# Four column tiles of 32 for the sums and the router's products, and the queries' high part on ScalarE

## Chip, cores and metric

The kernel runs on 1 core of a Trainium2 chip. The metric is the device time of one execution in microseconds (us), lower is better. Its engines are TensorE (PE; PEld is its weight load), VectorE (DVE), ScalarE (ACT), GpSimd (POOL) and SyncE (SP), which here issues most DMAs. Each engine runs its own instructions in program order and waits for the others through semaphores.

## The reference, cut to what matters

```python
# x, ctx: (4, 512, 512); 8 heads over the 512 positions, d = 64 positions each
xn  = layernorm(x)
q, k = l2norm over d of xn and ctx, per head
sm  = softmax(5.0 * einsum('bhdq,bhdk->bhqk', q, k))
x   = x + einsum('bhqk,bhdk->bhdq', sm, v)          # v = ctx
t   = layernorm(x).reshape(2048, 512)
logits = t @ Wg + bg                                 # 4 experts
# top 2 of 4, each expert keeps its 512 best tokens;
# out[sel] += (gelu(tok @ W1[i]) @ W2[i]) * p   for each expert i
return x + out
```

## The kernel before

The work has two phases. The attention phase goes through 16 units of 128 rows of `x` (two heads each). The expert phase (four experts, FP32 products made of three FP32R products of high and low parts) follows after a stretch that finds each expert's tokens. The change touches the attention phase alone.

A unit u passes through the engines in a software pipeline. In the body `unit(u, behind, ahead)` of each engine stand steps of units u-3 to u+3, written in a fixed order by hand; units 4 to 11 are a hardware loop of two bodies, the others are unrolled. `behind` and `ahead` say how many units lie before and after, up to 4 and 3. In the middle the orders are:

- PE: transpose the context of u+1 into `bank_t` (`values`, L1246), transpose the widened query norms of u+1 into `bank_m` (`spread_queries`, L1254), scores of u for key tiles 2 and 3 (L1267), weighted values 0 and 1 (L1277), transpose the normalized rows of u+2 into `bank_m`, transpose `x2n` of u-3 into `bank_t`, scores of u+1 for tiles 0 and 1, router logits of u-3 (L1305: four products, each with 128x128 weights `x2n_t` and 4 moving columns `wg`, into `bank_t`), weighted values 2 and 3, sums (L1289: four products of `half_sum` against 64 columns of ones, heads at rows 0 and 64 of `o_ps[1]`, two accumulated for each head).
- DVE: statistics of u+3, `queries(u+1)` (L823 `q_f`, L825 `q_hi`, then `x_norm` of u+2 at L788, then `q_lo` at L831), key squares of u+1, half sums 0, `invert_few(u-1)` (L844), query squares of u+2, half sums 1, residual and second statistics of u-2, `widen_queries(u+2)` (L837), `take_logits(u-3)` (L815), `normalize_x2(u-2)` (L892, waits for `rstd2` of POOL).
- ACT: sums of u-1 (L673), key squares and values of u+1 (L626, L633), four exponentials of u for tiles 2 and 3 (L653), query squares of u+2 (L618), `x2n_t` of u-3 (L679), four exponentials of u+1 for tiles 0 and 1, which wait for the key norms of POOL, key high part of u+2 (L643), output of u (L665).
- POOL: key norms of u+1, query norms of u+2, two inverse deviations, key low part.
- SP, in a ring over the unit: store `x2n` (L402), load `x_all` (L372) and `c_sb` (L377), two DMAs `few` (L410: one row of `p_sum` for each head, spread over 64 partitions of 8), wait for `few_inv` of DVE, store it to `inv_dram` (L412), two broadcasts back into `p_inv` (L415), store the output rows (L399, waits for DVE's residual).

`values(u+1)` on PE waits for `logit_done` (of u-4) in the middle units, since the logits stood in `bank_t`; `spread_queries` follows it.

Of the kernel before, what the change touches and what calls it, by code (L numbers as in the profile page):

```python
# [15 lines left out]
ALU = mybir.AluOpType  # L16
# [22 lines left out]
FEW = 2 * D // P  # L39
DVE_HEADS, POOL_HEADS = (0, 1), ()  # L40
# [28 lines left out]
C_ALL = C_RESET + E * 2 * UNITS  # L69


def constants():

    import numpy as np

    c = np.zeros((P, C_ALL), np.float32)
    p = np.arange(P)
    c[:, C_IDENT:C_IDENT + P] = np.eye(P)
    c[:, C_BEFORE:C_BEFORE + P] = (p[:, None] < p[None, :]) - 1.0
    c[:, C_ONES:C_ONES + P] = 1  # L80
    c[:, C_BLOCK:C_BLOCK + P] = p[:, None] // WAYS == p[None, :] // WAYS
# [8 lines left out]
    c[:, C_RESET:C_ALL] = np.arange(E * 2 * UNITS) % (2 * UNITS) != 0  # L90
    return c


def xattn_moe_kernel(nc, x, ctx_in, Wg, bg, W1, W2, consts, out):
# [6 lines left out]
    with ExitStack() as stack:  # L101
# [8 lines left out]
        wg = keep("wg", [P, KD, E])  # L110
# [59 lines left out]
        with ExitStack() as phase:  # L170
            def att(name, shape, dt=F32):
                return phase.enter_context(nc.sbuf_tensor(name, shape, dt))

            x_all = att("x_all", [P, UNITS, D])
            c_sb = [att(f"c_sb{n}", [P, D]) for n in range(2)]
            c_sq = att("c_sq", [P, D])
            x_norm = [att(f"x_norm{n}", [P, D]) for n in range(2)]
            x_sq = att("x_sq", [P, D])

            k_hi = [att(f"k_hi{n}", [P, D], F32R) for n in range(2)]  # L180
            k_lo = [att(f"k_lo{n}", [P, D], F32R) for n in range(2)]
# [8 lines left out]
            few = att("few", [P, FEW])  # L190
# [4 lines left out]
            x2n_t = att("x2n_t", [P, KD, P])  # L195
            stats = att("stats", [P, 6])
# [12 lines left out]
            wide_q = att("wide_q", [P, TT, 2, DH])  # L209
            power = att("power", [P, 16])  # L210
# [26 lines left out]
        wg_in = sem("wg_in")  # L237
        bg_in = sem("bg_in")
# [33 lines left out]
        few_in = sem("few_in")  # L272
        few_done = sem("few_done")
# [95 lines left out]
        def _(sp):  # L369
# [23 lines left out]
            sp.dma_start(wg[:, :, :], Wg.rearrange("(k p) e -> p k e", p=P)).then_inc(wg_in, 16)  # L393
# [10 lines left out]
            def spread_inverse(u):  # L404
# [3 lines left out]
                for h in range(2):  # L408
                    half = slice(h * P // 2, (h + 1) * P // 2)
                    sp.dma_start(few[half, :], p_sum[DH * h:DH * h + 1, :]).then_inc(few_in, 16)  # L410
# [63 lines left out]
        def _(pool):  # L474
# [3 lines left out]
            nc.gpsimd.memset(power[:, :], -0.5).then_inc(power_set, 1)  # L478
            pool.wait_ge(power_set, 1)
# [131 lines left out]
        def _(act):  # L611
# [32 lines left out]

            def exponentials(u, t, reused):
# [21 lines left out]
            def take_sums(u, reused):  # L667
# [3 lines left out]
                if reused:  # L671
                    act.wait_ge(few_in, 32 * n)
                nc.scalar.activation(p_sum[:, :], o_ps[1][:, :], ACT.Copy).then_inc(sum_taken, 1)  # L673

            def take_x2t(u, bank=bank_t):
# [4 lines left out]
                                     ACT.Copy).then_inc(x2t_taken, 1)  # L680

# [12 lines left out]
            round_keys((0, 1), False)  # L694
            act.wait_ge(rk_done, 1)
# [3 lines left out]
            def unit(u, behind, ahead):  # L699
# [5 lines left out]
                exponentials(u, 2, behind > 0)  # L705
                exponentials(u, 3, behind > 0)
# [4 lines left out]
                if ahead:  # L711
                    act.wait_ge(rk_done, number(u) + 2)
                    exponentials(after(u), 0, True)
                    exponentials(after(u), 1, True)
                if ahead > 1:
# [55 lines left out]
        def _(dve):  # L771
# [39 lines left out]
            def take_logits(u, bank=bank_t):  # L811
# [4 lines left out]
                                        bank[:, 0:E], bgb[:, :], ALU.add).then_inc(logit_done, 1)  # L816

            def queries(u, follow):
# [151 lines left out]
            def unit(u, behind, ahead):  # L970
# [27 lines left out]
                if behind > 2:  # L998
                    take_logits(before(before(before(u))))
# [15 lines left out]
            take_logits(before(before(end)))  # L1015
# [11 lines left out]
            take_logits(end)  # L1027
# [206 lines left out]
        def _(pe):  # L1234
# [46 lines left out]
            def sums(u, behind, ahead):  # L1281
# [5 lines left out]
                for n in range(2):  # L1287
                    for h in range(2):
                        last = nc.tensor.matmul(o_ps[1][DH * h:DH * (h + 1), :], cst[:, C_ONES:C_ONES + DH],  # L1289
                                                half_sum[h][n][:, :], start=(n == 0), stop=(n == 1))  # L1290
# [10 lines left out]
            def router_logits(u, bank=bank_t):  # L1301
# [18 lines left out]
            def unit(u, behind, ahead):  # L1320
# [16 lines left out]
                if ahead > 1:  # L1337
                    pe.wait_ge(qhi_done, n + 2)
                    transpose_queries(after(after(u)))
                if behind > 2:  # L1340
                    if ahead:
                        pe.wait_ge(v_taken, n + 2)
                    else:
                        pe.wait_ge(logit_done, n - 3)
# [26 lines left out]
            router_logits(before(before(end)))  # L1371
# [3 lines left out]
            router_logits(before(end), bank_m)  # L1375
            pe.wait_ge(logit_done, UNITS - 2)
            transpose_x2(end)
            router_logits(end)
# [126 lines left out]
```

## Time and profile before

| | us |
|---|---|
| median of 3 runs | 624.82 |
| lowest, highest | 622.26, 625.44 |
| the profiled execution, whole | 624.58 |
| its span, first to last instruction | 622.8 |
| mean granted TensorE clock in it | 0.957 of full |
| attention phase, roughly | 0 to 200 |
| expert phase, roughly | 262 to 622 |

The rows below come from the one profiled execution. Times are counted from the span's start. An engine's next short instruction can start a little before the last one's recorded end, so distances are taken from start to start. A row of the timeline that ends in a bracket tells how long the engine sat idle before it and what ended that. The name written `logits` in a row of DVE is `take_logits`.

### The profile page before, as it was taken

How to read it: one execution, taken by the hardware profiler on the slowest of the kernel's cores; microseconds unless marked ns; L12 is line 12 of the kernel's file. 1: busy time of each engine (PE TensorE's matmuls, PEld its weight loads, DVE VectorE, ACT ScalarE, POOL GpSimd, SP SyncE). 2: the span in 40 equal slices, each digit the busy share in tenths (PEclk: the TensorE clock that was granted, in tenths of full speed). 3: DMA queues.
4: the chain of work that ended last, by engine and by line, in shares of the span. 5: the costliest groups of instructions: out<-in, count | busy, mean ns of one | idle time of the engine just before them, and what ended most of it. 6: DMA issues, size and time to landing. Idle time of an engine off the chain costs nothing.

```text
span 622.8 us, 8726 instructions
## 1 busy us (share of the span) xinstructions
PE 568.2 (91%) x2842; PEld 408.5 (66%) x2842; DVE 354.3 (57%) x702; ACT 281.6 (45%) x421; POOL 187.0 (30%) x143
## 2 busy tenths in 40 slices
PE   3999999999998512999999999999999999999994
PEld 2545554554554401788888888888888788888883
DVE  5789998999888684443345443444633354423212
ACT  3777767767777130443333433334334324333220
POOL 8456566566551243100120330300510400500002
PEclk9999999999999655799999999999999999999998
DMA  4523423323213133323332543324451432542001
GB/s 146 196 60 119 137 86 118 126 94 109 96 53 118 52 115 96 95 100 128 97 113 88 183 149 120 118 84 134 152 184 69 137 124 76 190 149 68 0 1 67
DMA packets 46600, 67.73 MB, mean 109 GB/s; under 512 B 8560, under 2 KB 25072, under 8 KB 46576
## 3 DMA queue, kind: packets, MB, share of 16 engines
q1 hardware_dynamic: 42736, 54.84, 26.4%
q0 software_dynamic: 3840, 12.59, 6.2%
q8 instruction: 13, 0.21, 0.1%
q14 instruction: 11, 0.09, 0.0%
HBM read 54.70 MB, written 12.64 MB: 108 GB/s over the span
## 4 chain that ended last, share of the span: by engine, by line
PE 65%; DVE 5%; issue 4%; DMA 1%; POOL 1%; POOLq 0%; DVEq 0%; ACT 0%; SPq 0%
PE two L1423 29%; PE four L1453 9%; PE four L1452 9%; PE four L1450 9%; PE two L1277 2%; PE four L1267 2%; DVE junk L1046 1%; PE two L1289 1%; PE bank_t L1305 1%; DMA x_got<-x2n_dram,idx_all 1%; POOL w_lo L533 1%; DMA p_inv<-inv_dram 0%; PE bank_t L1411 0%; PE bank_m L1411 0%; DVE onehot L1133 0%
## 5 line engine op out<-in xcount | busy, mean ns | idle before, releaser
L759 ACT ACTIVATE h_f<-two 128x512 f32<-128x512 f32 x64 | 38.3, 599 | 231.2 <-PE two L1423 231.2
L1207 DVE TENSOR_TENSOR h_lo<-h_f,h_hi 128x512 fp32r<-128x512 f32 x64 | 44.1, 689 | 125.7 <-ACT h_hi L760 125.7
L1423 PE MATMUL two<-xt_hi,w_hi 128*128 (+1 forms) x256 | 102.9, 402 | 0.7 <-ACT xt_hi L748 0.7
L1423 PE MATMUL two<-xt_hi,w_lo 128*128 (+1 forms) x256 | 101.3, 396 | 0.0
L1453 PE MATMUL four<-w_hi,h_lo 128*128 128x512 f32 x256 | 100.5, 393 | 0.0
L1423 PE MATMUL two<-xt_lo,w_hi 128*128 (+1 forms) x256 | 100.5, 395 | 0.0
L1450 PE MATMUL four<-w_hi,h_hi 128*128 128x512 f32 x256 | 100.5, 392 | 0.0
L1452 PE MATMUL four<-w_lo,h_hi 128*128 128x512 f32 x256 | 100.4, 392 | 0.0
L653 ACT ACTIVATE prob<-four,rnorm 128x512 f32<-128x512 f32 x128 | 77.6, 688 | 28.6 <-POOL rnorm L476 17.6
L1177 DVE TENSOR_TENSOR w_lo<-raw,w_hi 128x2048 fp32r<-128x2048 f32 x30 | 68.7, 2290 | 23.3 <-ACT w_hi L686 23.3
L476 POOL TENSOR_TENSOR rnorm<-ss_max,power 128x8 f32<-128x8 f32 x32 | 64.7, 2024 | 51.5 <-DVE ss_max L808 45.3
L606 POOL DMA_INDIRECT out<-o_got,idx_all x16 | 20.2, 1264 | 165.4 <-DVE o_got L1228 163.0
L585 POOL DMA_INDIRECT x_got<-x2n_dram,idx_all x16 | 23.9, 1496 | 139.9 <-DVE idx_all L1164 125.1
L1277 PE MATMUL two<-prob,v_t 128*64 128x512 f32 x256 | 62.0, 605 | 0.0
L686 ACT ACTIVATE w_hi<-raw 128x2048 fp32r<-128x2048 f32 x32 | 61.3, 1918 | 0.0
L1423 PEld LDWEIGHTS two<-xt_hi,w_hi 128*128 128x128 f32 x256 | 48.6, 190 | 11.7 <-ACT xt_hi L748 1.1
L1423 PEld LDWEIGHTS two<-xt_hi,w_lo 128*128 128x128 f32 x256 | 48.6, 190 | 11.1
L1423 PEld LDWEIGHTS two<-xt_lo,w_hi 128*128 128x128 f32 x256 | 48.5, 189 | 10.7
L1450 PEld LDWEIGHTS four<-w_hi,h_hi 128*128 128x128 f32 x256 | 48.1, 188 | 10.9
L1453 PEld LDWEIGHTS four<-w_hi,h_lo 128*128 128x128 f32 x256 | 48.1, 188 | 10.8
L1452 PEld LDWEIGHTS four<-w_lo,h_hi 128*128 128x128 f32 x256 | 48.1, 188 | 10.6
L856 DVE TENSOR_TENSOR half_sum<-prob 128x512 f32<-128x512 f32 x64 | 41.5, 689 | 0.1
(177 smaller groups left out, 741.5 us busy)
## 6 DMA issues: line engine op xcount, KB each, us to landing
raw<-in_L_ffn_W SPq DMA_DIRECT2D x64, 512.0 KB, 4.0
x_all<-in_x SPq DMA_DIRECT2D x16, 256.0 KB, 2.9
c_sb<-in_ctx SPq DMA_DIRECT2D x16, 256.0 KB, 2.8
out<-x_all SPq DMA_DIRECT2D x16, 256.0 KB, 2.0
x2n_dram<-x2n SPq DMA_DIRECT2D x16, 256.0 KB, 2.0
p_inv<-inv_dram SPq DMA_DIRECT2D x30, 128.0 KB, 2.8
few<-p_sum SPq DMA_DIRECT2D x30, 2.0 KB, 2.2
cst<-in_consts SPq DMA_DIRECT2D x1, 354.5 KB, 5.0
```

Source lines behind the costliest of these rows:

```text
L476: return nc.gpsimd.tensor_tensor(dst, src, power[:, 0:n], ALU.pow)
L653: last = nc.scalar.activation(prob[h][t][:, :], s_ps[:, 2 * (t % 2) + h, :], ACT.Exp, scale=rnorm[u[1]][:, 0, t, h:h + 1])
L686: nc.scalar.activation(w_hi[c % SPLIT_BUFS][:, :], raw[c % RAW_BUFS][:, :], ACT.Copy).then_inc(whi_done, 1)
L759: nc.scalar.activation(h_f[m % 2][:, :], z_ps[m % 2][:, :], ACT.Gelu)
L856: nc.vector.tensor_tensor(half_sum[h][n][:, :], prob[h][2 * n][:, :], prob[h][2 * n + 1][:, :], ALU.add).then_inc(halves_done[h], 1)
L1177: nc.vector.tensor_tensor(w_lo[c % SPLIT_BUFS][:, :], raw[c % RAW_BUFS][:, :], w_hi[c % SPLIT_BUFS][:, :].bitcast(F32), ALU.subtract).then ...
L1207: nc.vector.tensor_tensor(h_lo[m % 2][:, :], h_f[m % 2][:, :], h_hi[m % 2][:, :].bitcast(F32), ALU.subtract).then_inc(h_split, 1)
L1277: last = nc.tensor.matmul(o_ps[0][DH * h:DH * (h + 1), :], v_t[u[1]][:, t, h, :], prob[h][t][:, :], start=(t == 0), stop=(t == TT - 1))
L1423: return nc.tensor.matmul(z[:, :], w_part[c][:, w], x_k, start=start, stop=stop)
L1450: nc.tensor.matmul(acc_ps[:, t, :], h_hi[m % 2][:, h], w_hi[c][:, w], start=(m == 0), stop=False)
L1452: nc.tensor.matmul(acc_ps[:, t, :], h_hi[m % 2][:, h], w_lo[c][:, w], start=False, stop=False)
L1453: last = nc.tensor.matmul(acc_ps[:, t, :], h_lo[m % 2][:, h], w_hi[c][:, w], start=False, stop=(m == MT - 1))
```

## The change

Three things are changed in the attention phase:

1. In units with `ahead`, the four sum products go to four column tiles of 32 (rows 0, 32, 64, 96 of `o_ps[1]`) with nothing accumulated. So each head has two partial sums: SP issues four `few` DMAs for two, DVE adds the two halves of `few` and then inverts.
2. The router's logits of the middle units: weights and moving data are swapped (`wg`, widened with zeros to 32 columns, is the weight, `x2n_t` moves, 128 columns), the four parts stand on four column tiles of `bank_m`; ACT copies them (`r_part`, 128x128), and one more product with the constant `C_QUAD` adds and transposes them into `bank_m`. They are placed around the sums, at the end of PE's body. `values` then waits for `x2t_taken`, and `spread_queries` for `logit_done`. In the last units the four products stay as they were (`router_whole`).
3. `q_hi` is no longer computed by DVE from `x_norm`: ACT copies `q_f`, between the exponentials of tiles 2 and 3. DVE normalizes u+2 before it waits for it.

```diff
@@ SP
-            sp.dma_start(wg[:, :, :], Wg.rearrange("(k p) e -> p k e", p=P)).then_inc(wg_in, 16)
+            sp.wait_ge(wg_clear, 1)
+            sp.dma_start(wg[:, :, 0:E], Wg.rearrange("(k p) e -> p k e", p=P)).then_inc(wg_in, 16)
...
                 for h in range(2):
                     half = slice(h * P // 2, (h + 1) * P // 2)
-                    sp.dma_start(few[half, :], p_sum[DH * h:DH * h + 1, :]).then_inc(few_in, 16)
+                    for m in range(2):
+                        row = QUAD * (2 * m + h)
+                        sp.dma_start(few[half, m * FEW:(m + 1) * FEW], p_sum[row:row + 1, :]).then_inc(few_in, 16)
@@ POOL
+            nc.gpsimd.memset(wg[:, :, :], 0.0).then_inc(wg_clear, 1)
@@ ACT
+            def round_queries(u):
+
+                act.wait_ge(q_done, number(u) + 1)
+                nc.scalar.activation(q_hi[u[1]][:, :], q_f[:, :], ACT.Copy).then_inc(qhi_done, 1)
+            def take_parts(u, bank=bank_m):
+
+                act.wait_ge(parts_ready, number(u) + 1)
+                nc.scalar.activation(r_part[:, :], bank[:, 0:P], ACT.Copy).then_inc(parts_taken, 1)
...
                 exponentials(u, 2, behind > 0)
+                if ahead:
+                    round_queries(after(u))
                 exponentials(u, 3, behind > 0)
...
                     exponentials(after(u), 1, True)
+                if behind > 2 and ahead:
+                    take_parts(before(before(before(u))))
@@ DVE
-                nc.vector.scalar_tensor_tensor(q_hi[u[1]][:, :], x_norm[u[1]][:, :], ALPHA, bank_m[:, :],
-                                               ALU.mult, ALU.mult).then_inc(qhi_done, 1)
+                if follow is not None:
+                    normalize(follow)
                 dve.wait_ge(q_done, n + 1)
                 dve.wait_ge(qhi_done, n + 1)
-                if follow is not None:
-                    normalize(follow)
                 nc.vector.tensor_tensor(q_lo[u[1]][:, :], q_f[:, :], q_hi[u[1]][:, :].bitcast(F32), ALU.subtract
                                         ).then_inc(q_split, 1)
...
-                dve.wait_ge(few_in, 32 * (n + 1))
-                nc.vector.reciprocal(few_inv[:, :], few[:, :]).then_inc(few_done, 1)
+                dve.wait_ge(few_in, 64 * (n + 1))
+                nc.vector.tensor_tensor(few_sum[:, :], few[:, 0:FEW], few[:, FEW:2 * FEW], ALU.add
+                                        ).then_inc(few_added, 1)
+                dve.wait_ge(few_added, n + 1)
+                nc.vector.reciprocal(few_inv[:, :], few_sum[:, :]).then_inc(few_done, 1)
@@ PE
+                        if ahead:
+
+                            row = QUAD * (2 * n + h)
+                            last = nc.tensor.matmul(o_ps[1][row:row + QUAD, :], cst[:, C_ONES:C_ONES + QUAD],
+                                                    half_sum[h][n][:, :], start=True, stop=True,
+                                                    tile_position=(0, row))
...
+            def router_parts(u, bank=bank_m):
 
                 pe.wait_ge(x2t_taken, number(u) + 1)
                 for k in range(KD):
-                    last = nc.tensor.matmul(bank[:, 0:E], x2n_t[:, k, :], wg[:, k, :],
+                    last = nc.tensor.matmul(bank[QUAD * k:QUAD * (k + 1), 0:P], wg[:, k, :], x2n_t[:, k, :],
+                                            start=True, stop=True, tile_position=(0, QUAD * k))
+                last.then_inc(parts_ready, 1)
+
+            def router_logits(u, bank=bank_m):
+
+                pe.wait_ge(parts_taken, number(u) + 1)
+                nc.tensor.matmul(bank[:, P:P + E], r_part[:, :], cst[:, C_QUAD:C_QUAD + E], start=True, stop=True
+                                 ).then_inc(logit_ready, 1)
...
                 if ahead:
                     if behind > 3:
-                        pe.wait_ge(logit_done, n - 3)
+                        pe.wait_ge(x2t_taken, n - 3)
                     else:
                         pe.wait_ge(v_taken, n + 1)
                     values(after(u))
+                    if behind > 3:
+                        pe.wait_ge(logit_done, n - 3)
                     spread_queries(after(u))
...
-                    pe.wait_ge(qhi_done, n + 2)
+                    pe.wait_ge(q_done, n + 2)
                     transpose_queries(after(after(u)))
...
-                if behind > 2:
-                    router_logits(before(before(before(u))))
+                if not ahead:
+                    router_whole(before(before(before(u))), bank_t)
                 weighted_values(u, 2)
                 weighted_values(u, 3)
+                if behind > 2 and ahead:
+                    pe.wait_ge(xsq_done, n + 3 if ahead > 1 else UNITS)
+                    router_parts(before(before(before(u))))
                 sums(u, behind, ahead)
+                if behind > 2 and ahead:
+                    router_logits(before(before(before(u))))
```

## Rows read from the trace of the kernel before

**Rows 1.** Windows: length, busy us (count) of PE, PEld, DVE, ACT, POOL; clock, DMA share, GB/s.
```profile
60.50:155.50 95.00, 93.90 (x580) 50.66 (x576) 86.58 (x218) 69.01 (x120) 57.23 (x40) 1.00 0.34 112
262.00:622.00 360.00, 351.95 (x1595) 286.63 (x1593) 142.79 (x152) 122.29 (x155) 55.66 (x40) 0.99 0.33 111
```

**Rows 2.** Timeline of DVE, one unit: start us, us, what, count, idle before.
```profile
120.21 0.16 DVE L815 TENSOR_TENSOR logits<-bank_t,bgb 128x4 f32 x1
...
120.83 0.55 DVE L892 TENSOR_SCALAR x2n<-x_all,mv,rstd 128x512 f32 x1 [0.47 <-POOL rstd L476]
...
122.31 0.68 DVE L823 SCALAR_TENSOR_TENSOR q_f<-x_norm,bank_m 128x512 f32<-128x512 f32 x1
122.91 0.68 DVE L825 SCALAR_TENSOR_TENSOR q_hi<-x_norm,bank_m 128x512 fp32r<-128x512 f32 x1
...
124.14 0.68 DVE L831 TENSOR_TENSOR q_lo<-q_f,q_hi 128x512 fp32r<-128x512 f32 x1
...
126.87 0.19 DVE L844 RECIPROCAL few_inv<-few 128x8 f32<-128x8 f32 x1
...
127.82 1.30 DVE L856 TENSOR_TENSOR half_sum<-prob 128x512 f32<-128x512 f32 x2
...
131.95 0.15 DVE L815 TENSOR_TENSOR logits<-bank_t,bgb 128x4 f32 x1
```

**Rows 3.** The same view, the unit before it.
```profile
108.20 0.15 DVE L815 TENSOR_TENSOR logits<-bank_t,bgb 128x4 f32 x1
...
112.42 0.68 DVE L831 TENSOR_TENSOR q_lo<-q_f,q_hi 128x512 fp32r<-128x512 f32 x1
```

**Rows 4.** Timeline of PE around the same unit.
```profile
115.59 1.05 PE L1305 MATMUL bank_t<-wg,x2n_t 128*128 128x4 f32 x8
...
118.34 1.89 PE L1289 MATMUL two<-half_sum,cst 128*64 128x512 f32 x8
120.50 0.65 PE L1246 MATMUL bank_t<-cst,c_sb 128*128 128x128 f32 x4 [0.27 <-DVE logits L815]
120.98 0.60 PE L1254 MATMUL bank_m<-cst,wide_q 128*128 128x128 f32 x4
121.51 0.51 PE L1267 MATMUL four<-q_hi,k_hi 64*128 64x512 f32 x2
```

**Rows 5.** Timeline of ACT in the same unit.
```profile
118.76 0.65 ACT L643 ACTIVATE k_hi<-c_sb 128x512 fp32r<-128x512 f32 x1
...
122.74 2.42 ACT L653 ACTIVATE prob<-four,rnorm 128x512 f32<-128x512 f32 x4 [0.47 <-PE four L1267]
...
128.18 2.42 ACT L653 ACTIVATE prob<-four,rnorm 128x512 f32<-128x512 f32 x4 [1.41 <-POOL rnorm L476]
```

**Rows 6.** Timeline of SP's DMA issues, both units.
```profile
111.52 1.14 SPq L410 DMA_DIRECT2D few<-p_sum  x2
...
123.29 1.13 SPq L410 DMA_DIRECT2D few<-p_sum  x2
```

**Rows 7.** Tile `few`, 60 to 156 us: issue ns min/median/max; DMA from issue to landing.
```profile
L410 SPq DMA_DIRECT2D few<-p_sum x16: 491/548/597, 64.2 to 147.6; - x16
...
DMA to landing us min/median/max: 2.0/2.3/2.5
```

**Rows 8.** The same tile, 168 to 192 us, where no inputs are loaded.
```profile
DMA to landing us min/median/max: 1.7/1.8/1.8
```

**Rows 9.** Timeline of DVE: first and last logits of the loop, the last units.
```profile
60.89 0.15 DVE L815 TENSOR_TENSOR logits<-bank_t,bgb 128x4 f32<-128x4 f32 x1
...
155.68 0.15 DVE L815 TENSOR_TENSOR logits<-bank_t,bgb 128x4 f32 x1
...
178.17 0.15 DVE L815 TENSOR_TENSOR logits<-bank_t,bgb 128x4 f32<-128x4 f32 x1
...
181.72 0.69 DVE L831 TENSOR_TENSOR q_lo<-q_f,q_hi 128x512 fp32r<-128x512 f32 x1
```

**Rows 10.** Timeline of ACT in a unit before the first logits.
```profile
45.52 1.84 ACT L653 ACTIVATE prob<-four,rnorm 128x512 f32<-128x512 f32 x3 [0.81 <-POOL rnorm L476]
```

More of the change, by code:

```diff
@@ L39 @@
 FEW = 2 * D // P
+QUAD = P // 4
 DVE_HEADS, POOL_HEADS = (0, 1), ()
@@ L68 @@
 C_RESET = C_SELF + E * E
-C_ALL = C_RESET + E * 2 * UNITS
+C_QUAD = C_RESET + E * 2 * UNITS
+C_ALL = C_QUAD + E
 def constants():
@@ L89, in constants @@
     c[:, C_SELF:C_SELF + E * E] = (j == i) * -1e30
-    c[:, C_RESET:C_ALL] = np.arange(E * 2 * UNITS) % (2 * UNITS) != 0
+    c[:, C_RESET:C_QUAD] = np.arange(E * 2 * UNITS) % (2 * UNITS) != 0
+    c[:, C_QUAD:C_ALL] = p[:, None] % QUAD == np.arange(E)[None, :]
     return c
@@ L109, in xattn_moe_kernel @@
         cst = keep("cst", [P, C_ALL])
-        wg = keep("wg", [P, KD, E])
+        wg = keep("wg", [P, KD, QUAD])
         bgb = keep("bgb", [P, E])
@@ L189, in xattn_moe_kernel @@
             half_sum = [[att(f"half_sum{h}{n}", [P, D]) for n in range(2)] for h in range(2)]
-            few = att("few", [P, FEW])
+            few = att("few", [P, 2 * FEW])
+            few_sum = att("few_sum", [P, FEW])
             few_inv = att("few_inv", [P, FEW])
@@ L195, in xattn_moe_kernel @@
             x2n_t = att("x2n_t", [P, KD, P])
+            r_part = att("r_part", [P, P])
             stats = att("stats", [P, 6])
@@ L237, in xattn_moe_kernel @@
         wg_in = sem("wg_in")
+        wg_clear = sem("wg_clear")
+        parts_ready = sem("parts_ready")
+        parts_taken = sem("parts_taken")
         bg_in = sem("bg_in")
@@ L272, in xattn_moe_kernel @@
         few_in = sem("few_in")
+        few_added = sem("few_added")
         few_done = sem("few_done")
@@ L671, in take_sums @@
                 if reused:
-                    act.wait_ge(few_in, 32 * n)
+                    act.wait_ge(few_in, 64 * n)
                 nc.scalar.activation(p_sum[:, :], o_ps[1][:, :], ACT.Copy).then_inc(sum_taken, 1)
@@ L694, in _ @@
             round_keys((0, 1), False)
+            round_queries((0, 0))
             act.wait_ge(rk_done, 1)
@@ L809, in sum_key_squares, with take_logits @@
                                         ).then_inc(ssk_floor, 1)
-            def take_logits(u, bank=bank_t):
+            def take_logits(u, bank=bank_m):
                 n = number(u)
@@ L815, in take_logits @@
                 nc.vector.tensor_tensor(logits[:, bass.ds(n, 1), :].rearrange("p a e -> p (a e)"),
-                                        bank[:, 0:E], bgb[:, :], ALU.add).then_inc(logit_done, 1)
+                                        bank[:, P:P + E], bgb[:, :], ALU.add).then_inc(logit_done, 1)
             def queries(u, follow):
@@ L998, in unit @@
                 if behind > 2:
-                    take_logits(before(before(before(u))))
+                    take_logits(before(before(before(u))), bank_m if ahead else bank_t)
                 if behind > 1 and ahead:
@@ L1014, in _ @@
             normalize_x2(before(end), True)
-            take_logits(before(before(end)))
+            take_logits(before(before(end)), bank_t)
             residual(end, 1)
@@ L1026, in _ @@
             put(nc.vector.scalar_tensor_tensor(rest0[:, :], count0[:, :], -2.0, excess[:, :], ALU.mult, ALU.add))
-            take_logits(end)
+            take_logits(end, bank_t)
             dve.wait_ge(logit_done, UNITS)
@@ L1288, in sums @@
                     for h in range(2):
-                        last = nc.tensor.matmul(o_ps[1][DH * h:DH * (h + 1), :], cst[:, C_ONES:C_ONES + DH],
-                                                half_sum[h][n][:, :], start=(n == 0), stop=(n == 1))
+                        if ahead:
[3 more added lines that the diff above has]
+                                                    tile_position=(0, row))
+                        else:
+                            last = nc.tensor.matmul(o_ps[1][DH * h:DH * (h + 1), :], cst[:, C_ONES:C_ONES + DH],
+                                                    half_sum[h][n][:, :], start=(n == 0), stop=(n == 1))
                 last.then_inc(sums_ready, 1)
@@ L1299, in transpose_x2, with router_whole @@
                 last.then_inc(x2t_ready, 1)
-            def router_logits(u, bank=bank_t):
+            def router_parts(u, bank=bank_m):
                 pe.wait_ge(x2t_taken, number(u) + 1)
                 for k in range(KD):
-                    last = nc.tensor.matmul(bank[:, 0:E], x2n_t[:, k, :], wg[:, k, :],
+                    last = nc.tensor.matmul(bank[QUAD * k:QUAD * (k + 1), 0:P], wg[:, k, :], x2n_t[:, k, :],
[5 more added lines that the diff above has]
+                                 ).then_inc(logit_ready, 1)
+            def router_whole(u, bank):
+                pe.wait_ge(x2t_taken, number(u) + 1)
+                for k in range(KD):
+                    last = nc.tensor.matmul(bank[:, P:P + E], x2n_t[:, k, :], wg[:, k, 0:E],
                                             start=(k == 0), stop=(k == KD - 1))
@@ L1343, in unit @@
                     else:
-                        pe.wait_ge(logit_done, n - 3)
+                        pe.wait_ge(x2t_taken, n - 3)
                     transpose_x2(before(before(before(u))))
@@ L1370, in _ @@
             transpose_x2(before(before(end)))
-            router_logits(before(before(end)))
+            router_whole(before(before(end)), bank_t)
             pe.wait_ge(exp_done, TT * UNITS)
@@ L1374, in _ @@
             transpose_x2(before(end), bank_m)
-            router_logits(before(end), bank_m)
+            router_whole(before(end), bank_m)
             pe.wait_ge(logit_done, UNITS - 2)
             transpose_x2(end)
-            router_logits(end)
+            router_whole(end, bank_t)
             transpose_keys(EARLY, UNITS, 2)
```

## The prediction

> **What bounds the kernel now.** I read the table of windows first, then the timelines of DVE, PE, ACT and SP over two units of the loop. The change touches only the attention phase; the expert phase, 360 us at a granted clock of 0.99, stays [rows 1]. In 95 us of the loop PE is busy 93.9 us and DVE 86.6 us [rows 1], so the table alone says "PE". The timelines say something else. From one `take_logits` to the next on DVE is 12.01 and 11.74 us (108.20, 120.21, 131.95) [rows 2, 3], on average (155.68 - 60.89) / 8 = 11.85 us [rows 9]. PE's `values` starts 0.29 us after `take_logits` of DVE and had been idle 0.27 us for it [rows 4]. Behind `take_logits` DVE has no idle time but 0.47 us at `x2n` for POOL [rows 2]: the busy share of 91% hides gaps between dependent instructions. So two rings of nearly equal length hold each other. A saving on PE alone is worth nothing beyond that 0.27; the unit gets shorter only if the ring through DVE does.
>
> I call the start of `take_logits` D, the start of `q_lo` Q. Before, D to Q is 4.22 and 3.93 us, Q to the next D 7.79 and 7.81 us [rows 2, 3].
>
> **The change part by part.**
>
> *Sums on four column tiles.* Eight passes on two tiles take about 1.8 us from start to end [rows 4]; on four tiles I take half, 0.9 us; bounds 0.9 (four abreast) and 1.8 (two abreast as now). Saved on PE: 0 to 0.9 us a unit.
>
> *Router.* The old four products take 1.05 us on PE [rows 4]. New: eight passes of 128 columns on four tiles, then one product with 4 columns. One old product is a quarter of 1.05, 0.26; I take 0.35 + 0.3 us, bounds 0.4 and 1.3 in all. ACT gets one more copy of 128x128, at most the 0.65 us of a 128x512 copy such as `k_hi` [rows 5]; I take 0.3.
>
> Together PE falls from about 11.7 to 10.4 us a unit: it stops being a bound. But its logits now come last in its body. They must be there when DVE is at D. Half sums 1 of DVE end 2.8 us before D (127.82 + 1.30 against 131.95) [rows 2]; after them PE needs the sums and one product, 1.2 us (2.1 at the upper bounds): ready 0.7 to 1.6 us early. ACT's `take_parts` stands behind the exponentials of u+1, which start 4.04 us after Q (128.18 against 124.14) [rows 2, 5] and last 2.42; with the copy, the product and two hand-overs that is Q + 7.2, against Q + 8.0 for D: hidden as well, by 0.8 us. Nothing of parts 1 and 2 on PE costs or gains.
>
> *The wait of `spread_queries`.* `values` no longer waits for D; `spread_queries` does. So the chain from D is now: 0.29 us to the spread (the distance that D to `values` has now), 0.53 to the scores of tile 2 (120.98 to 121.51), 1.23 from there to the exponentials (121.51 to 122.74) [rows 4, 5]. The exponentials of tile 2 start at D + 2.05, where they were at D + 2.53.
>
> *`q_hi` on ACT.* DVE loses 0.60 us (122.31 to 122.91, q_f to q_hi) [rows 2]. But the copy stands behind the two exponentials of tile 2 on ACT. Two of four that last 2.42 us take 1.16 until the next can start, the copy like `k_hi` 0.65 [rows 5], the hand-over to DVE some 0.05. `q_hi` is there at 2.05 + 1.16 + 0.65 + 0.05 = D + 3.91. `q_f` ends at about D + 2.8 and `x_norm` at D + 3.3, so DVE is ready some 0.6 us too early and sits. D to Q becomes 3.91, in place of 4.22 and 3.93: of the 0.60 saved, 0.17 is left on average. Behind the waiting `q_lo` on DVE is the whole rest of the body, and behind Q POOL's key norms. The exponentials of tile 3 start 0.53 us later, which only WV 2 and 3 of PE and half sums 1 need, both microseconds later.
>
> *The addition of `few`.* One 128x8 instruction more and a wait for it: about 0.19 for such an instruction (`few_inv`) [rows 2], 0.20 with the gap. It lies on DVE's path. Q to D becomes 7.80 + 0.20 = 8.00. So far a unit is 3.91 + 8.00 = 11.91 us, against 11.85: nothing gained.
>
> *Two more `few` DMAs.* SP issues them behind the store of `x2n` and the two loads; the first `few` starts at D + 3.32 and D + 3.08 [rows 2, 3, 6]. One issue takes 0.49 to 0.60 us [rows 7] and two take 1.14 [rows 6], so the fourth starts 1.80 us after the first instead of 0.55. From issue to landing: 2.0 to 2.5 us in the loop [rows 7], 1.7 to 1.8 where no load is under way [rows 8]. The fourth comes as the loads are just ending, I take 2.0, bounds 1.7 and 2.5. All four are there at D + 3.32 + 3.80 = 7.12 and D + 6.88, and 0.05 for the wait. DVE stands at `invert_few` at Q + 2.73 (126.87 - 124.14) [rows 2], that is D + 6.64. It waits 0.53 and 0.29 us, 0.41 on average; bounds 0.1 and 0.9. Before, the second of two landed 0.7 us ahead of DVE. Nothing on DVE passes this wait: query squares, half sums 1, residual, `widen_queries` and D itself are behind it, and the next `x2n`, hence the next `few`, behind D. It closes a ring: 11.91 + 0.41 = 12.32 us a unit, +0.47.
>
> By "Issuing engines are not separate DMA queues" in *DMA: Bandwidth & Descriptors* of the Trainium skill, the time to initiate a DMA is usually small beside the DMA itself. Here an issue of 0.55 us stands against about 2 us; if it were nothing, the four would land with the second, no wait would arise, and the sum would be that of the first rival.
>
> *Edges.* The loop's eight distances: 8 x 0.47 = +3.8 us. The next unit still loads a context: +0.5. In the last two with logits there are no loads before `few`, so no wait for it, but DVE was not held by `q_hi` before: D to Q was 3.55 (178.17 to 181.72) [rows 9] and becomes 3.91, with the addition +0.56 each, 1.1 together. The tail behind them hangs on `few_inv` and is carried along. The first units have no logits. There a part of PE's saving could show (at most 3 x 0.9 us), yet their exponentials of u+1 already wait 0.81 us for POOL's norm [rows 10], which is behind Q, and Q moves back by about 1.1 us against the spread: I take +0.3, bounds -2 and +1. POOL's memset of `wg` and SP's wait for it: under 0.1 us beside loads, nothing.
>
> Sum: 3.8 + 0.5 + 1.1 + 0.3 = +5.7 us. The profiled execution took 624.58 us whole (622.8 span and 1.8 around it), 0.2 under the median: 624.6 + 5.7 = 630.3 us.
>
> **The rivals.**
> 1. *No wait for `few`.* The two later DMAs land in 1.7 us or less from issue, or issue faster. Then a unit is 11.91: 8 x 0.06 = 0.5, the next +0.3, +1.1 and +0.3: 626.8 us. For it: 1.7 where the queues are empty [rows 8]. Against it: `c_sb` is issued only 0.5 us before `few`, and landings in the loop are 2.0 and more [rows 7].
> 2. *A larger wait.* Four `few` of 64 small pieces each hold one another up in the queues, landing 2.5 us after issue: wait 0.9, a unit 12.8, 624.6 + 8 x 0.97 + 2.3 = 634.7 us.
> 3. *Faster.* The hold-up at `q_lo` is not there, because ACT comes to the exponentials of tile 2 earlier than my chain allows, and `few` is there in time. Then DVE's balance decides: -0.60 - 0.2 (the gap ahead of `x_norm` in every second unit, 0.1 on average) + 0.20, about -0.45 a unit over 12 units: 619 us. Against it: the chain D, spread, scores, exponentials, copy, `q_lo` is written out in program order on each engine, and every piece has a row. A reader of the busy table would go further and take off PE's whole 1.3 us a unit, 609 us; DVE's ring does not allow that. *TensorEngine Tiling (Array Packing)*, "Theoretical Speedup", of the Trainium skill promises up to 4x for 32 columns; by that rule and a PE bound it would be this 609. No row of the kernel before has four tiles.
> 4. *The tiles don't run abreast.* If the four 32-column products run one after another, the sums take 3.6 us rather than 0.9, with the product and its hand-overs 4.0 us behind half sums 1, logits are ready 1.2 us after DVE wants them, a unit is about 13.1: 624.6 + 12 x 1.25 = 640 us. It decides once sums and logits last over 2.8 us together. Against it: two tiles already overlap, eight passes recorded as 0.59 us each in 1.89 [rows 4].
>
> **How the numbers follow.** Forecast (few-wait of 0.2 to 0.7) 0.50; rival 1: 0.25; rival 2: 0.13; rival 3: 0.09; rival 4: 0.03. The likeliest gives 630.3. Its own range is 628 to 633 (wait bounds, and the edges). The range of 8 in 10 takes in rival 1 down to 625.5 and most of rival 2: 625.5 to 634.5. 0.5% is 3.1 us, about what a measurement of this kernel can tell from no change: slower means over 627.9. Slower: 0.50 less 0.03, 0.13, 0.03: 0.63. Faster, under 621.7: 0.09, and the rest 0.28 is within.
>
> **What would show it.** In the changed kernel: `take_logits` to `take_logits` near 12.3 us; ahead of `q_lo` DVE idle 0.5 to 0.7 us, released by ACT `q_hi`; ahead of `few_sum` idle 0.3 to 0.5, released by the DMA; PE busy less, with idle time ahead of `spread_queries`, released by DVE's logits; sums in 0.9 us. It is wrong if DVE has no idle time at `q_lo`, if PE waits for nothing, or if `take_logits` itself waits for PE.

## The result, and the profile after

| | before | changed |
|---|---|---|
| median, us | 623.81 (4 runs) | 630.18 (4 runs) |
| lowest, highest | 622.26, 625.44 | 629.30, 630.52 |
| span of the profiled execution | 622.8 | 628.4 |
| mean granted TensorE clock | 0.957 | 0.955 |

The ratio is 1.0101, 95% interval 1.0077 to 1.0125: slower by 1.0%. The forecast was 630.3 us. One execution among all those below, of the kernel with the sums alone, took 952.74 us at a mean granted clock of 0.559 of full and is left out of that kernel's figures.

The engines of the changed kernel, from its page (busy us, share of the span, instructions). Before, PE was busy 568.2 us, DVE 354.3 and ACT 281.6.

```profile
PE 556.8 (89%) x2866; PEld 395.9 (63%) x2866; DVE 348.1 (55%) x701; ACT 288.5 (46%) x449; POOL 187.1 (30%) x144
```

TensorE does 11.4 us less and VectorE 6.2 us less, and the kernel is 5.6 us longer. The next line is the loop in the table of windows, as [rows 1] show it of the kernel before. From the first to the last of the nine `take_logits` that bound eight units it takes 99.4 us, against 94.8 before, and PE is busy 88.9 us of it, against 93.7.

```profile
61.60:161.00 99.40, 88.90 (x592) 43.74 (x592) 83.64 (x217) 72.62 (x137) 57.15 (x41) 0.98 0.33 108
```

The timeline of DVE over one unit of the changed kernel, as [rows 2, 3] show it of the kernel before:

```profile
112.41 0.15 DVE L843 TENSOR_TENSOR logits<-bank_m,bgb 128x4 f32 x1
...
114.67 0.69 DVE L851 SCALAR_TENSOR_TENSOR q_f<-x_norm,bank_m 128x512 f32<-128x512 f32 x1
115.28 0.54 DVE L816 TENSOR_SCALAR x_norm<-x_all,mv,rstd 128x512 f32 x1
116.41 0.69 DVE L857 TENSOR_TENSOR q_lo<-q_f,q_hi 128x512 fp32r<-128x512 f32 x1 [0.59 <-ACT q_hi L661]
...
119.43 0.17 DVE L870 TENSOR_TENSOR few_sum<-few 128x8 f32<-128x8 f32 x1 [0.22 <-DMA few<-p_sum]
119.64 0.20 DVE L873 RECIPROCAL few_inv<-few_sum 128x8 f32<-128x8 f32 x1
...
124.72 0.15 DVE L843 TENSOR_TENSOR logits<-bank_m,bgb 128x4 f32 x1
```

Where `q_hi` was computed, DVE now sits idle 0.59 us for ACT's copy of it, and further down 0.22 us for the `few` DMAs. ACT in the same stretch shows why: the copy comes when two exponentials are through, and those had waited 1.09 us for PE's scores.

```profile
114.52 1.27 ACT L671 ACTIVATE prob<-four,rnorm 128x512 f32<-128x512 f32 x2 [1.09 <-PE four L1296]
115.68 0.63 ACT L661 ACTIVATE q_hi<-q_f 128x512 fp32r<-128x512 f32 x1
116.20 1.27 ACT L671 ACTIVATE prob<-four,rnorm 128x512 f32<-128x512 f32 x2
```

PE at the end of that unit, against [rows 4]: the parts on four tiles, the sums on four, the adding product, `values`, and the spread, which now waits 0.99 us for DVE's logits (0.47 us in the unit before).

```profile
121.22 0.43 PE L1341 MATMUL bank_m<-x2n_t,wg 128*32 128x128 f32 x8
121.99 1.07 PE L1321 MATMUL two<-half_sum,cst 128*32 128x512 f32 x8 [0.35 <-issue]
123.09 0.39 PE L1348 MATMUL bank_m<-cst,r_part 128*128 128x4 f32 x2
123.33 0.63 PE L1275 MATMUL bank_t<-cst,c_sb 128*128 128x128 f32 x4
124.95 0.63 PE L1283 MATMUL bank_m<-cst,wide_q 128*128 128x128 f32 x4 [0.99 <-DVE logits L843]
```

So TensorE's saving arrived as work saved, 0.8 us in the sums (1.07 for 1.89) and some 0.2 in the router (0.43 and 0.39 for 1.05), and became idle time, most of it ahead of the spread. A second ring, through SyncE, is about as long as that through the copy of `q_hi`. In the stretch of 112 to 125 us the chain that the profile follows back, at each step to what ended its wait, runs there: from `x2n` through SyncE's queue and the last of the four DMAs to `few_sum`. In order of time (start, us, what):

```profile
112.95 0.56 DVE x2n L921
113.52 0.34 SPq L412
...
115.82 0.51 SPq L422
...
117.64 1.77 DMA few<-p_sum
119.43 0.18 DVE few_sum L870
...
124.72 0.17 DVE logits L843
```

One unit of the loop, its first, is an outlier: 14.12 us from `take_logits` to `take_logits` (61.62 to 75.74), with a wait of 2.03 us at `few_sum`.

```profile
70.45 0.17 DVE L870 TENSOR_TENSOR few_sum<-few 128x8 f32<-128x8 f32 x1 [2.03 <-DMA few<-p_sum]
```

In the sum of differences, changed minus before, by the starts of `take_logits`:

| stretch | before | changed | difference | forecast |
|---|---|---|---|---|
| start to the first of the loop | 60.89 | 61.62 | +0.7 | +0.3 |
| the outlier unit | 11.79 | 14.12 | +2.3 | +0.5 |
| seven other units | 83.00 | 85.27 | +2.3 | +3.3 |
| next unit | 11.32 | 11.60 | +0.3 | +0.5 |
| next two | 21.08 | 21.77 | +0.7 | +1.1 |
| the rest | 434.70 | 434.05 | -0.6 | 0 |
| span | 622.78 | 628.43 | +5.6 | +5.7 |

### The profile page after: what moved, and what is told of

Read it like the earlier page. It is cut to its first block, busy times and chain, and to the rows that moved or that the text cites. A ratio compares the mean times of both kernels' runs of the same rounds, so it can differ in the third digit from the quotient of the medians.

```text
span 628.4 us, 8855 instructions
## 1 busy us (share of the span) xinstructions
PE 556.8 (89%) x2866; PEld 395.9 (63%) x2866; DVE 348.1 (55%) x701; ACT 288.5 (46%) x449; POOL 187.1 (30%) x144
## 4 chain that ended last, share of the span: by engine, by line
PE 62%; DVE 11%; issue 9%; POOL 7%; DMA 3%; ACT 3%; SPq 3%; POOLq 0%; DVEq 0%; ACTq 0%
PE two L1480 29%; PE four L1510 9%; PE four L1509 9%; PE four L1507 9%; POOL rnorm L488 3%; POOL rstd L488 2%; DMA few<-p_sum 2%; ACT prob L671 2%; SPq L422 2%; PE four L1296 1%; DVE q_lo L857 1%; DVE half_sum L885 1%; DVE junk L1075 1%; ACT q_hi L661 1%; DVE ss L833 1%
## 5 line engine op out<-in xcount | busy, mean ns | idle before, releaser
L671 ACT ACTIVATE prob<-four,rnorm 128x512 f32<-128x512 f32 x128 | 79.5, 692 | 42.6 <-POOL rnorm L488 19.2
L1480 PEld LDWEIGHTS two<-xt_hi,w_hi 128*128 128x128 f32 x256 | 48.6, 190 | 11.7 <-issue 1.1
```

The costliest lines, as they stand in the source:

```text
L671: last = nc.scalar.activation(prob[h][t][:, :], s_ps[:, 2 * (t % 2) + h, :], ACT.Exp, scale=rnorm[u[1]][:, 0, t, h:h + 1])
L1480: return nc.tensor.matmul(z[:, :], w_part[c][:, w], x_k, start=start, stop=stop)
```

## The experiments

My theory: DVE's ring sets the unit. From D (`take_logits`) to Q (`q_lo`) it is held by the copy on ACT, from Q to D by DVE's own work with the addition, now and then by the `few` DMAs; PE is no bound. The rivals: PE's saving does count and something else ate it; or the loss is all in the DMAs; or all in the copy. The fences below show the main lines of each edit, cut at "...". Each kernel ran beside the kernel before, and each ratio is against it.

### One part undone

**Part 1 undone**: two tiles, two DMAs, no addition.

```diff
-                    for m in range(2):
-                        row = QUAD * (2 * m + h)
-                        sp.dma_start(few[half, m * FEW:(m + 1) * FEW], p_sum[row:row + 1, :]).then_inc(few_in, 16)
+                    sp.dma_start(few[half, 0:FEW], p_sum[DH * h:DH * h + 1, :]).then_inc(few_in, 16)
...
-                nc.vector.tensor_tensor(few_sum[:, :], few[:, 0:FEW], few[:, FEW:2 * FEW], ALU.add
...
-                        if ahead:
+                        if False:
```

> The changed kernel with part 1 undone: sums on two tiles, two few DMAs, no addition on DVE; router and ScalarE copy as changed. Theory (DVE's ring, with few, sets the unit): the wait of DVE ahead of few_inv is gone and so is the addition of 0.20 us, though PE's sums take 1.8 us again instead of 1.0. take_logits to take_logits about 11.75 us in the loop (12.14 and one of 14.12 in the changed kernel), time 624.7 us (623.5 to 626). Rival (PE's saving did count, and something else was lost): 0.8 us more on PE a unit show, 12.9 us a unit, about 638 us.

Measured: 627.26 us (626.6 to 627.66), ratio 1.0051 (1.0030 to 1.0071). A unit of the loop is 11.85 us on average (62.53 to 157.31), not 12.42 as in the changed kernel, and DVE never waits for `few`: the rival's 12.9 is excluded. But the time is 2.6 us over my figure and outside my range. The loop begins 0.9 us later than in the changed kernel (62.53 against 61.62) and the last units with logits take 11.44 and 10.97 us where those of the changed kernel take 11.39 and 10.38. In these edges PE is a bound and its longer sums show: DVE waits 0.80 us for the adding product of PE ahead of the last of these `take_logits` (at 191.12 us), and 0.04 us in the changed kernel.

**Part 3 undone**: `q_hi` by DVE.

```diff
-                if follow is not None:
-                    normalize(follow)
+                nc.vector.scalar_tensor_tensor(q_hi[u[1]][:, :], x_norm[u[1]][:, :], ALPHA, bank_m[:, :],
+                                               ALU.mult, ALU.mult).then_inc(qhi_done, 1)
...
-                if ahead:
-                    round_queries(after(u))
```

> The changed kernel with part 3 undone: DVE computes q_hi again, sums and router as changed. Theory: DVE does 0.60 us more but no longer waits 0.6 us for ScalarE, take_logits to q_lo 4.22 and 3.93 us in turn (4.00 and 3.89 in the changed kernel), a unit about 12.1 us, time 629.5 us (628 to 631), so about as the changed kernel. Rival (moving q_hi off DVE is a gain of 0.6 us a unit): 12.7 us a unit, 637 us. Rival (the copy is the whole loss): 624 us.

Measured: 629.06 us (626.45 to 629.52), ratio 1.0069 (1.0045 to 1.0094). D to Q 4.21 and 3.93, a unit 12.31 and 11.99 us. In the loop, DVE with 0.60 us more to do takes just as long as DVE that waits for the copy:

```profile
121.14 0.15 DVE L840 TENSOR_TENSOR logits<-bank_m,bgb 128x4 f32 x1
125.07 0.68 DVE L856 TENSOR_TENSOR q_lo<-q_f,q_hi 128x512 fp32r<-128x512 f32 x1
127.84 0.17 DVE L869 TENSOR_TENSOR few_sum<-few 128x8 f32<-128x8 f32 x1
133.13 0.15 DVE L840 TENSOR_TENSOR logits<-bank_m,bgb 128x4 f32 x1
```

**Part 2 undone**: the router and the wait of `values` as before.

```diff
-                        pe.wait_ge(x2t_taken, n - 3)
+                        pe.wait_ge(logit_done, n - 3)
...
                     values(after(u))
-                    if behind > 3:
-                        pe.wait_ge(logit_done, n - 3)
```

> The changed kernel with part 2 undone: the four router products as before, values waits for logit_done again; sums and ScalarE copy as changed. Theory: the queries' spread starts 0.78 us after take_logits instead of 0.29, so the exponentials and the copy behind them come 0.5 us later: take_logits to q_lo 4.4 us, a unit 12.4 us, few is there in time, time 632 us (630.5 to 634): the router's part is the one that helps. Rival (the router's extra copy and product cost something): 628 us or less.

Measured: 633.98 us (633.38 to 634.11), ratio 1.0160 (1.0134 to 1.0186). D to Q 4.40 to 4.42, every unit 12.41 to 12.43 us. DVE's wait at `q_lo` grows from 0.66 to 1.17 us, by as much as the spread comes later (it starts 0.78 us after D, not 0.29):

```profile
124.03 0.16 DVE L841 TENSOR_TENSOR logits<-bank_t,bgb 128x4 f32 x1
128.43 0.69 DVE L855 TENSOR_TENSOR q_lo<-q_f,q_hi 128x512 fp32r<-128x512 f32 x1 [1.17 <-ACT q_hi L661]
131.17 0.15 DVE L868 TENSOR_TENSOR few_sum<-few 128x8 f32<-128x8 f32 x1
```

In its profile the loop is as long as that of the changed kernel, 99.4 us: each unit is 0.24 us longer than a usual one there (12.42 for 12.18), 1.9 us over eight units, but it has no outlier. What the two profiles differ by lies outside the loop, most of it in the last three units with logits (36.15 us for 33.37), and 1.03 us of that is a wait for `few` (at 169.16 us), so not all of it is the spread.

### One part alone

These are the kernel before with one part of the change, made by undoing the two others as in the diffs above (for the router's part undone, the four old products and their place too).

> Part 1 alone on the kernel before: four column tiles for the sums, four few DMAs, the addition; router and q_hi as before. Theory: PE's saving shows only in the first units (about -0.8 us), then a unit is 4.08 + 8.00 = 12.08 us (11.85 before), and 0.2 us more in each of the last: 626.5 us (625 to 628). Rival (PE bound before): 12 x 0.8 less, 615 us.

Measured: 628.10 us (627.7 to 629.01), ratio 1.0068 (1.0048 to 1.0088). The loop begins at 59.74 us (60.89 before), then a unit is 12.18 us on average. PE is busy 0.7 us a unit less in the loop (88.0 us of eight units for 93.7) and the unit gets longer, not shorter: PE did not bound the loop of the kernel before. The addition and, in single units, a wait for `few` (0.32, and 1.00 in one of the last) cost more than I had allowed, 1.6 us over my figure and just outside my range.

> Part 2 alone on the kernel before: router parts on four tiles, the copy and the adding product; sums and q_hi as before. Theory: DVE's ring is unchanged, 11.85 us a unit; time 623.5 us (622 to 625), no difference that can be told. Rival (PE bound before): 0.4 us a unit less, 619 us. Rival (logits late at the end of PE's body): DVE idle ahead of take_logits, over 627 us.

Measured: 625.03 us (623.47 to 625.57), ratio 1.0012 (1.0000 to 1.0025). That is at the upper end of my range, 0.03 us outside it. A unit stays at 11.85 us. The router's products are recorded 0.2 us shorter, but PE's busy time in the loop hardly falls (93.57 us for 93.69), so this run alone says little on what PE's time is worth; the sums alone say it. The logits at the end of PE's body do hold up DVE in the last two units, where it has little to do:

```profile
177.32 0.16 DVE L838 TENSOR_TENSOR logits<-bank_m,bgb 128x4 f32<-128x4 f32 x1 [0.89 <-PE bank_m L1342]
188.28 0.16 DVE L838 TENSOR_TENSOR logits<-bank_m,bgb 128x4 f32<-128x4 f32 x1 [2.20 <-PE bank_m L1342]
```

> Part 3 alone on the kernel before: ScalarE copies q_hi between the exponentials; sums and router as before. Theory: without the earlier spread of part 2 the exponentials start 2.53 us after take_logits, q_lo at 4.4 us, a unit 12.2 us, and the first units later by 1.5 us: 632 us (630 to 633.5), the one part that costs most. Rival (0.6 us less for DVE is a gain): 620 us or less.

Measured: 630.25 us (629.56 to 631.22), ratio 1.0096 (1.0075 to 1.0117); D to Q 4.42 and 4.53, a unit 12.21 and 12.35 us. In medians the three alone cost 3.8, 0.7 and 5.9 us, 10.4 together, each against a median of 624.33; the whole change costs 6.4. The difference is part 2: alone it gives nothing, beside the copy it brings the spread forward and gives back about 4 us. The run with part 1 undone shows it in the loop: with parts 2 and 3 a unit is 11.85 us, with the copy alone 12.32. The run with part 2 undone costs 3.8 us more than the changed kernel.

### Is TensorE a bound in the changed kernel?

```diff
-                for n in range(2):
+                for n in (0, 1, 0, 1) if ahead else range(2):
```

> The changed kernel with the four sum products on PE issued twice over (same result, PE 0.9 to 1.0 us longer in each unit with ahead). Theory (PE is no bound in the changed kernel, its logits are ready about 1 us before DVE takes them): 630.2 us, within 1.5 us. Rival (PE counts): 12 units by 0.9 us, 641 us.

Measured: 631.35 us (630.02 to 632.05), ratio 1.0117 (1.0100 to 1.0134), where the changed kernel had 1.0101. The sums take 1.92 us instead of 1.07, and the spread's wait for DVE falls from 0.99 to 0.22 us:

```profile
123.08 1.92 PE L1321 MATMUL two<-half_sum,cst 128*32 128x512 f32 x16 [0.36 <-issue]
124.94 0.39 PE L1348 MATMUL bank_m<-cst,r_part 128*128 128x4 f32 x2
125.18 0.64 PE L1275 MATMUL bank_t<-cst,c_sb 128*128 128x128 f32 x4
126.04 0.64 PE L1283 MATMUL bank_m<-cst,wide_q 128*128 128x128 f32 x4 [0.22 <-DVE logits L843]
```

A unit is 12.32 and 12.01 us, as before the doubling. 0.85 us a unit of PE's time are free in the loop. What the doubling costs lies at the edges, where the loop begins at 63.26 us (61.62) and DVE waits 0.44 us for PE at the last `take_logits` of these units. The outlier is there again, in the same unit: 13.58 us with a wait of 1.49 us for `few`.

### Is it the place of the copy?

One step later on ACT, behind the exponentials of tile 3:

```diff
                 exponentials(u, 2, behind > 0)
-                if ahead:
-                    round_queries(after(u))
                 exponentials(u, 3, behind > 0)
+                if ahead:
+                    round_queries(after(u))
```

> The changed kernel with ScalarE's copy q_hi one step later, behind the exponentials of tile 3. Theory (the place of the copy on ScalarE sets q_lo): take_logits to q_lo goes from 3.95 to 5.1 us, a unit to 13.1 us, few in time, time about 640 us (637 to 643). Rival (q_lo's wait is covered by slack elsewhere): within 1 us of 630.

Measured: 644.48 us (two executions, 643.52 and 645.44), ratio 1.0333 (1.0312 to 1.0354). D to Q 5.15 and 5.06, a unit 13.14 and 13.08 us: D to Q is longer by 1.15 and 1.17 us, and two exponentials take 1.16 [rows 5]. The time is 4.5 us over my figure and outside my range; nearly all of it lies in the first units, which I had not counted: the loop begins at 65.53 us, not at 61.62.

```profile
117.97 0.15 DVE L843 TENSOR_TENSOR logits<-bank_m,bgb 128x4 f32 x1
123.11 0.69 DVE L857 TENSOR_TENSOR q_lo<-q_f,q_hi 128x512 fp32r<-128x512 f32 x1 [1.73 <-ACT q_hi L661]
```

### Is it the two more DMAs?

SyncE issues `few` behind the store of the output rows, ahead of the `x2n` store and the loads.

```diff
+                if follow is not None:
+                    issue_few(follow)
                 sp.wait_ge(x2n_done, n + 1)
                 sp.dma_start(x2n_dram[bass.ds(n * P, P), :], x2n[u[1]][:, :]).then_inc(x2n_stored[u[1]], 16)
```

> The changed kernel, but SyncE issues the four few DMAs before the store of x2n and the two loads. Theory: the wait ahead of few_sum is gone (0.22 us in every second unit, and the one of 2.03 us), every unit about 11.95 us, time 627.5 us (626.5 to 629): the two longer DMAs cost 2.5 to 3 us of the 6, the rest is the addition and the wait for q_hi. Rival (the few DMAs are the whole loss): 624.5 us. Rival (later loads stall something else): over 630 us.

Measured: 627.38 us (626.89 to 627.92), ratio 1.0058 (1.0038 to 1.0079). There is no wait at `few_sum` in any unit, nor an outlier: all are 11.91 to 12.00 us. By the ratios, 1.0058 and 1.0101, the place of the DMAs costs about 0.4% of the 1.0%. Single `few` land late here too (2.88 and 3.37 us), and DVE waits for none of them: issued early, they have the time.

```profile
121.59 0.15 DVE L851 TENSOR_TENSOR logits<-bank_m,bgb 128x4 f32 x1
125.48 0.69 DVE L865 TENSOR_TENSOR q_lo<-q_f,q_hi 128x512 fp32r<-128x512 f32 x1 [0.65 <-ACT q_hi L669]
128.22 0.15 DVE L878 TENSOR_TENSOR few_sum<-few 128x8 f32<-128x8 f32 x1
133.50 0.15 DVE L851 TENSOR_TENSOR logits<-bank_m,bgb 128x4 f32 x1
```

### A version that beats both

If the place of the copy is what holds DVE, then the copy ahead of the exponentials of tile 2 should let it go:

`few` stays first.

```diff
+                if ahead:
+                    round_queries(after(u))
                 exponentials(u, 2, behind > 0)
-                if ahead:
-                    round_queries(after(u))
                 exponentials(u, 3, behind > 0)
```

> few first as in the run of that name, and ScalarE's copy q_hi ahead of the exponentials of tile 2 instead of between them. It then starts when q_f is done, at 2.9 us after take_logits, and q_lo at 3.6 us. Theory: a unit about 11.65 us, time 624 us (622.5 to 626), about that of the kernel before. Rival (the exponentials, 1.4 us later, hold up PE or the next exponentials): 627 us or more.

Measured: 619.51 us (618.66 to 620.85), ratio 0.9931 (0.9918 to 0.9945): 0.7% faster than the kernel before. D to Q is 3.55 and 3.72, a unit 11.57 and 11.72 us, 11.62 on average, as expected. ACT now waits for `q_f` and not DVE for the exponentials; DVE's idle time ahead of `q_lo` is 0.31 us.

```profile
108.34 0.63 ACT L669 ACTIVATE q_hi<-q_f 128x512 fp32r<-128x512 f32 x1 [1.89 <-DVE q_f L859]
108.88 2.41 ACT L679 ACTIVATE prob<-four,rnorm 128x512 f32<-128x512 f32 x4
```

It is 4.5 us faster than my figure and outside my range, and that is again the edges: the loop begins at 58.95 us (61.80 with `few` first alone) and the last two units with logits take 10.38 and 9.95 us (11.39 and 10.38). The copy first without `few` first was not run.

The same with part 1 undone as above:

> The same with part 1 undone: two tiles, two few DMAs, no addition. Theory: 0.20 us less on DVE's ring, a unit about 11.45 us, time 621.5 us (620 to 623.5), faster than the kernel before by about 0.5%. Rival (with two tiles PE's 11.3 us of work are again the bound, or the tiles were worth it): 624 us or more.

Measured: 621.62 us (621.42 to 623.22), ratio 0.9970 (0.9960 to 0.9980). The number is as expected, but its reason is in part the rival: DVE now waits for PE's logits in every unit, 0.17 to 0.50 us.

```profile
118.79 0.16 DVE L849 TENSOR_TENSOR logits<-bank_m,bgb 128x4 f32 x1 [0.31 <-PE bank_m L1351]
```

A unit is 11.54 us on average. With DVE's ring shortened PE is the bound of the loop, busy in all of it. The loop with two tiles and that with four, in the table of windows:

```profile
61.01:153.35 92.34, 92.34 (x595) 45.15 (x595) 82.33 (x209) 73.72 (x137) 57.39 (x41) 1.00 0.35 115
58.95:151.92 92.97, 85.97 (x592) 43.02 (x592) 82.98 (x217) 71.82 (x138) 57.14 (x41) 1.00 0.36 115
```

In the loop four tiles don't pay even here: 11.62 us a unit for 11.54, with PE 6.4 us less busy and DVE's addition in its place. As whole kernels the ratios are 0.9931 (0.9918 to 0.9945) with four tiles and 0.9970 without, and that gain is in the edges: the loop begins 2.1 us earlier (58.95 for 61.01), and the last two units with logits take 10.38 and 9.95 us for 11.39 and 10.96.

And with part 2 undone instead:

> The version with few first and the copy ahead of tile 2's exponentials, with part 2 undone (router and the wait of values as before). Theory: the copy now starts when DVE's q_f is done, no matter when the exponentials could start, so the earlier spread is worth nothing: a unit 11.65 us, 620 us (618.5 to 621.5), as the version with part 2 (619.5). Rival (part 2 is needed for PE or the spread): 623 us or more.

Measured: 620.86 us (619.42 to 621.54), ratio 0.9941 (0.9918 to 0.9964), a unit 11.56 and 11.71 us. With the copy first, the earlier spread is worth nothing in the loop. Its interval overlaps that of the version with part 2 (0.9918 to 0.9945), so these runs don't tell whether part 2 gives anything there. A version with the copy first and both parts 1 and 2 undone was not run.

## Why the prediction was right, point by point

- **Two rings of nearly equal length, and PE's saving worth nothing in the loop.** Right. PE's work fell less than forecast: the sums took 1.07 us for a forecast 0.9, the router 0.43 and 0.39 for 0.35 and 0.3, and PE's busy time in a usual unit fell from 11.7 to 11.0 us, where I had 10.4. That it was worth nothing in the loop held: the sums alone made the loop longer, and sums twice over changed nothing in it. "Theoretical Speedup" in *TensorEngine Tiling (Array Packing)* of the Trainium skill allows up to 4x for 32 columns and up to 2x for 64, so up to twice as fast from one to the other. The trace comes near it: 1.07 against 1.89 us, 1.8 times.
- **D to Q 3.91 us.** Right: 3.89 to 3.90 in every second unit and 3.98 to 4.00 in the others, but for 4.20 in the one behind the outlier. The step that I took most care over, from the spread through the scores and two exponentials to the copy, held with each piece; the later copy added the two exponentials and the earlier one took them off. In the others the spread starts 0.06 us later after D (112.41 to 112.70 against 124.72 to 124.95) and the exponentials 0.10 later; I had one figure for both kinds of unit.
- **Q to D 8.00 us.** Right: with `few` first, where nothing waits at `few_sum`, it is 8.02 us (125.48 to 133.50). In the changed kernel it is 5.29 us from `few_sum` to `take_logits` (119.43 to 124.72), where it was 5.08 from `few_inv` before [rows 2].
- **The wait for `few`, 0.53 and 0.29 us.** The mechanism is right, the size was not: 0.21 to 0.23 us in every second unit and next to none in the others. The term mis-sized is the landing. I took 2.0 us for the fourth DMA, it was 1.8 (1.77 in the chain above), as where no inputs are loaded [rows 8]; the fourth was issued 1.82 us after the first (115.82 to 117.64), where I had 1.80. So a usual unit is 12.18 us (85.27 / 7) rather than 12.32. The trace does not bear out the rule cited from *DMA: Bandwidth & Descriptors* of the Trainium skill, that the time to initiate a DMA is usually small beside the DMA itself: one issue took 0.51 to 0.60 us, about a third of the landing of 1.8, and the issues ahead of the fourth took as long as its landing.
- **The outlier of 2.03 us** is not in the prediction. It brought back what the smaller waits had left out, and more: seven units +2.3 us for +3.3, the eighth +2.3 for +0.5. The agreement within 0.2 us of the whole is in that part luck: with a usual unit of 12.18 us in its place the profiled execution of 630.52 us would have been 1.9 us shorter, 628.6.
- **The first rival** (no wait for `few`, 626.8 us) did not come true, but the run with `few` issued first has no wait either and measured 627.38.
- **The edges.** The first units came out at +0.7 for +0.3, inside the bounds of -2 and +1. The runs with the copy late, the copy first and two tiles showed that the first units follow both PE and the copy, with differences of up to 6.6 us between them (the loop begins at 58.95 to 65.53). I did not see that when I wrote the expectations of those runs.
- **That DVE never waits for PE at `take_logits`** held in the loop (there is one gap of 0.04 us, behind it at 194.38), and in the loop even with the sums twice over, which made PE 0.85 us later.

## To carry to other kernels

An engine that is busy 99% of a stretch need not bound it. Follow the ring of waits once around across the engines, by the start-to-start distances of the trace, and count what each edit takes off that ring. Work moved to an idle engine comes back when that engine's program order lets it: here a copy of 0.63 us had two exponentials ahead of it, and putting it ahead of them turned a loss of 0.6% (with `few` first) into a gain of 0.7%. Splitting a result over more tiles multiplies the small DMAs that collect it, and it matters where these stand in their queue: the same four, issued first, left no wait.

## What the runs showed of the hardware

Four products on column tiles of 32 do run abreast: eight passes over 512 columns in 1.07 us against 1.89 on tiles of 64, and sixteen in 1.92.

The long landings of `few` go with instruction loads. In the outlier, the fourth DMA took 3.5 us from issue to landing, and the DMA view of 67 to 71 us shows one packet of 16 KB on an instruction queue in it. The page of the kernel before counts 13 on that queue in the whole execution. Queue and kind, packets, MB, share of 16 engines:

```profile
q1 hardware_dynamic: 224, 0.01, 2.8%
q8 instruction: 1, 0.02, 1.4%
```

With part 3 undone, one `few` of 3.2 us near the loop's end has the same packet beside it, and DVE waits 1.37 us.

```profile
q1 hardware_dynamic: 295, 0.02, 5.4%
q8 instruction: 1, 0.02, 1.6%
...
165.32 0.17 DVE L869 TENSOR_TENSOR few_sum<-few 128x8 f32<-128x8 f32 x1 [1.37 <-DMA few<-p_sum]
```

In the traces of all these runs, each `few` of more than 2.8 us (the longest 4.0) had such a packet within about 2 us of its issue. The reverse does not hold: in the version with the copy first, part 2 undone, a packet started at 48.08 us and the `few` issued at 48.13 landed after 2.26 us. That such a packet sits in the same DMA engines and holds up pieces behind it is the natural reading; it was not tried by itself. Nor does the packet's own length explain all of it: in the outlier it took 0.9 us (1.4% of 16 engines over 4 us), and the landing was 1.7 us longer than usual.

In the outlier PE sat idle 2.16 us for DVE's half sums, and the granted clock of the next 5 us was 0.60 and 0.71 of full (1.2 GHz for part of it), in a loop that otherwise has 1.00. The sums took 1.94 us there for 1.07. An idle stretch alone doesn't settle it: in the outlier of the run with the sums twice over PE sat idle 1.61 us, and the clock of that unit was 1.00.

```profile
72.50:74.90 2.40, 1.89 (x9) 0.26 (x9) 2.21 (x5) 0.85 (x2) 2.26 (x2) 0.60 0.34 96
74.90:77.50 2.60, 2.60 (x19) 2.35 (x18) 2.05 (x8) 1.64 (x3) 1.18 (x2) 0.71 0.29 113
```
